# Grouped convolution with per-pixel weights: the order of TensorE's tiles at the edges of the rounds, and the arithmetic of the last tile

## The reference

```python
B, IN_C, OUT_C, K, S, H, W = (8, 64, 64, 3, 8, 48, 48)
sel = jax.nn.softmax(conv_1x1(x, coupler_w) + coupler_b, axis=1)
sel = sel / sel.sum(axis=1, keepdims=True)
conv = conv_3x3(x, w).reshape(b_, s, oc, h_, w_) + bias
return jnp.einsum('bschw,bshw->bchw', conv, sel)
# and around it: x + that(_gn(x))
```

## Time and profile before

| what | value |
|---|---|
| time, median of 3 executions | 340.92 us (340.84 to 341.65) |
| the profiled execution: its own time | 341.6 us |
| its span, from the first to the last instruction | 339.8 us |
| busy: TensorE | 324.7 us (96%) |
| busy: VectorE | 277.7 us (82%) |
| busy: GpSimd | 229.5 us (68%) |
| busy: ScalarE | 109.2 us (32%) |

### The profile page before, as it was taken

How to read it: one execution, slowest core, us unless ns; L and a number is a source line. 1 busy time by engine, 2 the same in 40 slices (tenths; PEclk the granted TensorE clock), 3 DMA queues, 4 the chain that set the end, 5 groups by cost and what they waited for, 6 DMA issues and landing times.

```text
span 339.8 us, 5413 instructions
## 1 busy us (share of the span) xinstructions
PE 324.7 (96%) x1684; PEld 152.7 (45%) x1684; DVE 277.7 (82%) x504; ACT 109.2 (32%) x159; POOL 229.5 (68%) x329
## 2 busy tenths in 40 slices
PE   8996999999998999999999999999999899999993
PEld 8433444445443444445444444444544344444441
DVE  2799899997799688887799688887799687777786
ACT  1688251176111162175221062175221011111110
POOL 3700788899984598899854599899854599434343
PEclk9999899999999999999999999999999999999999
DMA  6799399019940695019950595019820596011002
GB/s 214 292 265 215 76 215 224 7 41 243 244 115 0 168 214 119 3 42 237 206 154 3 152 218 128 0 35 236 179 49 0 146 221 134 0 38 31 3 1 69
DMA packets 30374, 41.93 MB, mean 123 GB/s; under 512 B 2128, under 2 KB 23248, under 8 KB 29968
## 3 DMA queue, kind: packets, MB, share of 16 engines
q1 hardware_dynamic: 29184, 37.78, 46.0%
q10 hardware_dynamic: 1168, 3.89, 3.9%
HBM read 12.56 MB, written 4.72 MB: 51 GB/s over the span
## 4 chain that ended last, share of the span: by engine, by line
PE 69%; DVE 19%; issue 4%; DMA 4%; POOL 2%; SPq 1%; ACT 1%; DVEq 1%; ACTq 0%
PE pair L398 42%; PE pair L410 14%; PE pair L406 10%; DVE high L823 4%; DVE pair L822 3%; DVE half L831 3%; DVE pair L806 2%; DVE pair L808 2%; DMA op<-v_tail 2%; DMA x_raw<-x 2%; POOL v_pts L1112 2%; PE side L388 1%; DVE mix L790 0%; DVE v_pts L996 0%; DVE top L780 0%
## 5 line engine op out<-in xcount | busy, mean ns | idle before, releaser
L398 PE MATMUL pair<-w_head,op 128*128 128x512 f16 x864 | 234.9, 381 | 6.8 <-DVE half L831 3.5
L398 PEld LDWEIGHTS pair<-w_head,op 128*128 128x128 f16 x864 | 83.5, 98 | 110.6 <-DVE half L831 8.5
L410 PE MATMUL pair<-w_tail,op 128*128 128x512 f16 x288 | 109.4, 380 | 0.0
L594 ACT ACTIVATE m_sb<-pair 128x512 f32<-128x512 f32 x72 | 42.9, 596 | 200.6 <-PE pair L410 194.0
L1135 POOL TENSOR_TENSOR quarter<-half 128x256 f32<-128x256 f32 x71 | 52.8, 744 | 65.9 <-DVE half L831 65.3
L822 DVE TENSOR_TENSOR pair<-pair,sel_now 128x512 f32<-128x512 f32 x71 | 49.4, 696 | 38.9 <-PE pair L410 38.9
L831 DVE TENSOR_TENSOR half<-pair,high 128x512 f32<-128x512 f32 x71 | 49.1, 692 | 10.2 <-DVE high L823 1.0
L406 PE MATMUL pair<-w_tail,op_two 128*128 128x512 f16 x144 | 54.9, 381 | 0.0
L806 DVE TENSOR_TENSOR pair<-pair,m_sb 128x512 f32<-128x512 f32 x72 | 49.6, 689 | 0.0
L808 DVE TENSOR_TENSOR pair<-m_sb,pair 128x512 f32<-128x512 f32 x72 | 49.3, 684 | 0.0
L823 DVE TENSOR_TENSOR high<-pair,sel_now 128x512 f32<-128x512 f32 x71 | 48.3, 680 | 0.0
(11 more groups left out here) (110 smaller groups left out, 197.4 us busy)
## 6 DMA issues: line engine op xcount, KB each, us to landing
op<-v_head SPq DMA_DIRECT2D x14, 600.0 KB, 8.0
x_res<-x_pix SPq DMA_DIRECT2D x8, 576.0 KB, 6.5
op_two<-v_head SPq DMA_DIRECT2D x14, 300.0 KB, 9.0
op<-v_tail SPq DMA_DIRECT2D x14, 300.0 KB, 6.8
op<-v_head SPq DMA_DIRECT2D x14, 288.0 KB, 8.4
out<-y_out SPq DMA_DIRECT2D x7, 576.0 KB, 4.0
x_raw<-x ACTq DMA_DIRECT2D x3, 1152.0 KB, 9.2
w_raw<-weight SPq DMA_DIRECT2D x3, 768.0 KB, 8.8
```

What stands on the lines that cost most here:

```text
L398: nc.tensor.matmul(dst, op[b][:, 0, j, at + r * PW:at + r * PW + P], w_head[:, j, r, :], start=fresh and r == 0, stop=False, skip_group_ch ...
L410: return nc.tensor.matmul(dst, op[b][:, 1, j, at:at + P], w_tail[:, j, 0, :], start=False, stop=True, skip_group_check=True)
L594: act.activation(m1_sb[:, i % LOOK, :], pair[i % SETS_OF_BANKS][:, 0, :], ACT.Copy).then_inc(m1_copied, 1)
```

## The change

1. In TensorE's `round_`, `first_points(2)` of the next round is no longer issued at the end of a round. It stands behind `last_points(0)`, where the rule of the other tiles puts it. The order at an edge becomes: last 17, first 1', last 0', first 2', last 1', first 3'. Round 0 stays as it is, since there the first three tiles have been begun ahead of it.
2. In the last tile, pixel 0's product of 512 numbers goes to ScalarE: eight ACTIVATEs of 64 numbers, one for each set, with the weight as the scale (`last_products`). They start when `y_done` has been raised for pixel 0. VectorE keeps the product of pixel 1.
3. In the last tile, the three sums of each pixel become one `tensor_reduce` over the sets. Its input is read as (channel, set), so that neighbouring elements of the instruction's innermost axis lie 64 numbers of 4 bytes apart in `last_prod`. The additions of the input stay. The buffer `last_quarter` goes, and the numbers for which SyncE waits are fitted.

```diff
@@ TensorE, round_
                 for i in range(TILES):
                     last_points(i, n, begin)
-                    if 0 < i < TILES - 2:
+                    if i < TILES - 2 and not (begin and i == 0):
                         first_points(i + 2, n, begin and i + 2 == FIRST_TILES)
                     elif i >= TILES - 2 and more:
                         first_points(i + 2 - TILES, n + 1)
...
-                if more:
-                    first_points(2, n + 1)
-
@@ ScalarE
+            def last_products(n):
+
+                i = TILES - 1
+                act.wait_ge(sel_copied, n + 1)
+                act.wait_ge(y_done, n * 2 * TILES + 2 * i + 1)
+                for k in range(SETS):
+                    act.activation(last_prod[:, 0, k, :], pair[i % SETS_OF_BANKS][:, 0, k * C:(k + 1) * C], ACT.Copy,
+                                   scale=sel_w[:, 2 * i, k:k + 1]).then_inc(last_steps[0], 1)
...
                 round_(n, n + 1 < ROUNDS, n + 2 < ROUNDS)
+            last_products(ROUNDS - 1)
@@ VectorE, last_tile
-                hf = half[:, i % LOOK, :, :, :]
-                dve.wait_ge(half_used, n * TILES + i + 1)
                 dve.wait_ge(xb_done, (n * 2 + b + 1) * BIAS_PARTS)
                 dve.wait_ge(stored[b], n * 16 + 16)
-                def product(a):
...
-                product(0)
-                to_four(0)
-                product(1)
-                to_two(0)
-                to_four(1)
-                to_one(0)
-                to_two(1)
-                result(0)
-                to_one(1)
-                result(1)
+                dve.wait_ge(y_done, n * 2 * TILES + 2 * i + 2)
+                dve.tensor_tensor(last_prod[:, 1, :, :],
+                                  pair[i % SETS_OF_BANKS][:, 1, :].rearrange("p (s c) -> p s c", c=C),
+                                  spread(sel_w[:, 2 * i + 1, :], C), ALU.mult).then_inc(last_steps[1], 1)
+                for a in range(2):
+                    dve.wait_ge(last_steps[a], (SETS, 1)[a])
+                    dve.tensor_reduce(last_mixed[:, a, :], last_prod[:, a, :, :].rearrange("p s c -> p c s"),
+                                      axis=AX.X, op=ALU.add).then_inc(last_steps[a], 1)
+                for a in range(2):
+                    dve.wait_ge(last_steps[a], (SETS, 1)[a] + 1)
                     dve.tensor_tensor(y_out[b][:, t, a, :], last_mixed[:, a, :], x_res[b][:, t, a, :], ALU.add) \
                         .then_inc(last_steps[a], 1)
```

More of the change, by code:

```diff
@@ L160, in program @@
         last_prod = sb("last_prod", [P, 2, SETS, C])
-        last_quarter = sb("last_quarter", [P, 2, SETS // 4, C])
         last_mixed = sb("last_mixed", [P, 2, C])
@@ L357, in round_ @@
                     for a in range(2):
-                        wait(last_steps[a], 5)
+                        wait(last_steps[a], (SETS, 1)[a] + 2)
                     last_store()
```

## The result

| what | before | changed |
|---|---|---|
| time, median | 341.20 us (4 executions, 340.84 to 341.65) | 336.75 us (4 executions, 336.73 to 337.13) |
| ratio, with its 95% interval | | 0.9865 (0.985 to 0.9881) |
| the profiled execution: span, own time | 339.8, 341.6 us | 335.3, 337.13 us |

The changed kernel is 4.45 us, or 1.3%, faster by these medians. The forecast was 5.3 us and 335.6 us, with a range of 335.0 to 338.0.

The account below looks back on a forecast made before the run. TensorE, busy for 96% of the span, was taken as the bound, so only its waits and what follows its last matmul count. Edges 4.4 + last tile 0.9 = 5.3 us, from 340.92 to 335.6 us; range 335.0 to 338.0.

Parts of the forecast that it names:

- The halts go, 4.4 us: At the three round edges, TensorE's halts for VectorE's `halve` vanish under the new order, 4.4 us gained.
- step by step proof of the forecast: Edges: VectorE delivers in time, at the first with 0.38 us to spare for `halve(17)` and 0.6 for `halve(0')`.
- `multiply(0')` begins 0.2 us behind the copy: First edge, VectorE: the copy of the weights ends at 112.19 and `multiply(0')` was let start at 112.4.
- rival with VectorE: Edges: halts return if VectorE takes longer before `multiply(0')`; half back 337.8 us, chance 0.12; wholly back 340.0 us, chance 0.04.
- ScalarE's eight products, 1.8 us: Last tile: pixel 0's eight products on ScalarE take 1.8 us, upper bound 2.4, and are there at 335.3.
- The reduction, 0.68 us: Last tile, VectorE: a strided `tensor_reduce` of 512 elements was taken at 0.68 us, with 1.47 as the bound.
- first rival: Last tile: strided reduction costs two to three times the contiguous, 1.07 or 1.47 us; whole 336.3 to 337.1 us; chance 0.26.
- SyncE behind tile 16's store as the next bound, 0.9 us at most: Last tile: SyncE, free at 337.03 after issuing tile 16's store, limits the gain to 0.9 us.
- The sum: Whole kernel: 4.4 us from the edges and 0.9 from the last tile make 5.3 us, giving 335.6 us.
- The clock: TensorE: granted clock expected at 0.9 or more in every slice after the first edge.
- rival that was slower than before: TensorE's clock falls to 1.2 GHz in unbroken work; with 15 us there the time is 343.1 us; chance 0.04.

Follow-up runs that it names:

- e1: The kernel before with only the change of TensorE's `round_` (new order at the edges), last tile as before; 337.09 us, ratio 0.9872.
- f2: The changed kernel with six more copies of `sel_next` behind the copy of the weights, making VectorE late at the edges; 342.23 us, ratio 1.0021.
- the ladder: The changed kernel with fourteen added reductions of 512 numbers behind its last result, summed numbers 1 to 64 apart; 346.76 us, one execution.
- g1: The changed kernel with `last_prod` stored in pairs of channels, so reductions read 8 bytes apart; 336.18 us, ratio 0.9844.
- the e runs: First follow-up group: edges alone, last tile alone, the changed kernel again, and reductions over neighbours; before had a median of 341.6 us beside them.
- e3: The changed kernel once more, unchanged, as the yardstick; 336.89 us, ratio 0.987.
- e4: The changed kernel with `last_prod` stored as channel, set: reductions read neighbours, products are written 32 bytes apart; 336.44 us, ratio 0.9856.

## Why the prediction was right, and where its size was off

**The halts go, 4.4 us.** Right: 4.50 us in the long stretch, and e1 shows them without the rest. The step by step proof of the forecast held to hundredths: 0.39 and 0.60 us to spare at the first edge against 0.38 and 0.6, 1.51 and 1.69 us for `halve(0')` at the others against 1.5, and nothing new that is late.

**`multiply(0')` begins 0.2 us behind the copy.** It was idle for 0.25 us at the first edge, against 2.85 us before. The rival with VectorE fell with it, and f2 showed the point from which it would have decided.

**ScalarE's eight products, 1.8 us.** 1.74 us, 0.2 us apart. They ended with pixel 1's product on VectorE, as worked out, and the first reduction started at the moment forecast: 331.20 - 330.02 = 1.18 us behind the last matmul's start, against 335.31 - 334.15 = 1.16.

**The reduction, 0.68 us.** This is the term that was mis-sized. It took 1.01 and 1.00 us, the last store came 0.73 us behind SyncE's issue of tile 16's and not 0.1, and the tail gained 0.34 in place of 0.9 us. The prediction had the cost as its first rival, and its lower price, 1.07 us if only half of what L508 pays is for the read, was close. I chose the row of the same operation and engine over the row with the wide stride; the stride was the property that mattered. The step at 16 bytes is what the Trainium skill's page cited there ("SBUF — State Buffer", section "Door 1: The DMA port swizzle") would have told, with one correction: it lets 32-bit numbers be strided freely up to four of them, and at four, 16 bytes, the ladder shows 1.05 us. Only 4 and 8 bytes are shown to be free (12 was not tried).

**SyncE behind tile 16's store as the next bound, 0.9 us at most.** Right, as g1 shows: with reductions of 0.68 us the tail is 0.92 us shorter and the store waits for SyncE, 0.16 us and not 0.1 behind tile 16's. VectorE is only 0.07 us from bounding it too.

**The sum.** In the profiled executions 4.50 + 0.34 = 4.84 us are gained and the opening gives 0.37 back, which is the difference of the spans, 4.5 us. By medians it is 4.45 us here and 341.6 - 336.89 = 4.71 beside the e runs. So the 336.75 us lie where the first rival had them, 336.3 to 337.1, and above the forecast's 335.6. Of the 1.15 us between, 0.56 are the reductions and 0.28 the starting point: the forecast went down from 340.92 us, and the median of before here is 341.20. The range held because it took that rival in.

The opening varies by 1.1 us between executions of any kernel here, so a few tenths between trace and medians stay open. The traces show two things that differ in it: the granted clock from 20 to 36 us, 0.83 to 1.00 over the runs, and how long TensorE waits for a transfer into `op`, 2.25 to 3.32 us. The longest is that of the changed kernel's first profile (first row); before has 2.41 us, and e3, the same kernel again, has the second row:

```profile
33.23 1.35 PE L397 MATMUL pair<-w_head,op 128*128 128x512 f16 x3 [3.32 <-DMA op<-v_tail]
32.22 1.46 PE L397 MATMUL pair<-w_head,op 128*128 128x512 f16 x3 [2.32 <-DMA op<-v_tail]
```

Neither was varied by itself, so what each makes of the 0.37 us is not shown.

**The clock.** It stayed at 1.00 through 246.72 us of unbroken matmuls. The rival that was slower than before did not come.

## What to carry to other kernels

Where an engine halts at the seam of a loop, write down for each wait when its work ends and when the new order would ask for it; a proof of a few tenths of slack was enough here, and it also tells how much later work may be put there. A price from the row of the same instruction holds only if its access pattern is the same: look for the stride before the operation. Where both a write and a read need to be cheap, keep pairs of neighbours together, so that one side goes on by pairs and the other steps by 8 bytes.

## What the runs showed of the hardware that I had not expected

- VectorE's reads of 32-bit numbers in SBUF step in cost between 8 and 16 bytes from one element to the next: a reduction of 512 numbers 0.68 to 1.0 us. A product written 32 bytes apart takes 1.08 us in place of 0.69; where the step lies for writes was not tried. Pairs of neighbours cost nothing in either direction.
- A VectorE copy of 324 numbers takes 0.32 us alone and up to 1.15 us beside GpSimd's `input_and_bias`. Four of the six copies of f2 at its first edge, the last row behind that stretch:

```profile
111.42 0.61 DVE L869 COPY late<-sel_next 128x324 f32<-128x324 f32 x1
111.96 0.95 DVE L869 COPY late<-sel_next 128x324 f32<-128x324 f32 x1
112.83 1.15 DVE L869 COPY late<-sel_next 128x324 f32<-128x324 f32 x1
113.90 0.32 DVE L869 COPY late<-sel_next 128x324 f32<-128x324 f32 x1
```

  GpSimd is at work on L1106 and L1111 from 111.81 to 113.79 there. This is why the delay was 2.9 us and not 2.0.
- ScalarE's eight products start 0.2 us apart whether they write neighbours, 32 bytes apart or pairs, though each lasts longer with the stride (0.38 to 0.42 us in e4 against 0.31 to 0.36).
